# First stage of a two-layer convolution kernel: group statistics one quad later, batch sums between the spectral products, four result places

## The chip, the cores and the metric

The kernel runs on one core of one Trainium2 chip. The metric is the device time of one execution in microseconds (us); smaller is better. Before the change it is 5682.46 us, the median of three runs (5677.47 to 5682.60).

## The reference

`x` is (8, 128, 128, 128) in float32: eight batches of 128 images of 128 by 128. Two layers are computed, each adding to its input a function of the group-normalised input (32 groups of 4 images, so one group is one "quad"):

```python
x = x + filtered_lrelu(gn(x), f)      # layer 0: up by 2 with a 12-tap filter, leaky ReLU, filter and down by 2, in h and w
x = x + spectral(gn(x), a, b, c, d)   # layer 1: rfft2, product of low modes with a tensor-train weight, irfft2
def gn(v):                            # groups of 4 channels
    return (g - mean(g)) / sqrt(var(g) + 1e-5)
```

In layer 1 the kernel takes the mean and the scale of a group from sums over the batch's x1 (the output of layer 0) and puts them into the spectra after the transform.

## The kernel before, in words

There are three phases. The change touches only the first, `phase1`: it computes layer 0 and the forward spectra, and ends at about 3090 us of the span. The second multiplies the modes, the third transforms back and adds.

`phase1` handles one quad per step, 256 steps numbered q, with buffers chosen by k = q mod 8. Each engine has its own instruction list, written out by hand for eight steps (`body`) and looped by `steps`; engines meet only at semaphores, and each works strictly in the order of its list. So whatever one instruction waits for, all behind it on that engine waits too.

In step q TensorE (`step` in the block of `pe`) does, in this order: `up_cols` 0 and 1 of quad q; `down_rows` of quad q-1 (48 matmuls on Y, then six on Yt); `tails` (products with Yb, Yc, At); `up_rows` 0 of quad q+1, which needs g of quad q+1 (`g_ok`); `up_cols` 2 and 3 of q; `up_rows` 1 of q+1; `down_cols` of q-1; and the row transform of x1 of quad q-2 (products with `dfth`). PSUM is a ring of four pairs of banks; `pair_of(k, u)` says which pair the u-th piece uses. I count times of a step from the start of its `down_rows`.

ScalarE (`act`) copies from PSUM: `sloped` (L), `At`, `Yb`, Z high, `high(1)` (Y), Lt, Zt, A high, Yt, `sloped`, `high(3)`, A high, then G. VectorE (`dve`) computes Yf 0 and 1, Yc (`y_tail`), the statistics of x1 (L668), Z low, Zt low, Ytf, A low 0 (L638), Yf 2 and 3, A low 1, x1b (L709). GpSimd (`pool`) does `high(0)`, `low(0)`, `low(1)`, Yt, `high(2)`, `low(2)`, `low(3)`, and then `ground`, which writes g of quad q+2. `low(1)` waits for `high(1)` of ScalarE.

The group statistics of layer 0 are made for four quads at once, a "half" (HALF = 4). In the steps with k mod 4 = 0 and 1, `x_stats` runs bn_stats on x. At the end of k mod 4 = 1, `x_sums` (four small VectorE instructions, L572 to L578) prepares them. In k mod 4 = 2, TensorE sums over partitions (L359, before `tails`), VectorE reads the result (`stats_copy`, L583, before A low 0), forms the variance (`stats_var`, L588 to L592, after Yf 3), ScalarE takes the root (L460), and VectorE writes rstd and nmr (`stats_out`, L598 and L600, after A low 1). `ground` at the end of that step then makes g of the first quad of the next half.

Once per batch (step k = 5 of the last `body` of a batch, s6 given) the statistics of x1 are reduced: `batch_in` (L608 to L615), TensorE's sums L364, `batch_out` (L621 to L632), and after the step `spectra`: 16 units, each of eight matmuls with G (L418, L420), a copy psb by ScalarE (L528), two results by VectorE (L724, L726) into `sp_out`, and two stores of 256 KB by SyncE (L184). `sp_out` has two places; the copy psb waits for `batch_out`.

Of the kernel before, what the change touches and what calls it, by code (L numbers as in the profile page):

```python
# [28 lines left out]
IMGS = 4  # L29
# [11 lines left out]
X_SCALE = 128.0  # L41
# [23 lines left out]
def phase1(nc, x, ut_d, dt_d, dtail_d, mask_d, dfth_d, dftw_d, ones_d, x1, spec):  # L65
    with ExitStack() as ctx:
# [37 lines left out]
        sp_out = sb("sp_out", [128, 2, 2, 4, 128])  # L104
# [19 lines left out]
        sp_st = [sem("sp_st0"), sem("sp_st1")]  # L124
# [43 lines left out]
        def _(sp):  # L168
# [9 lines left out]
            def store_spectra(b):  # L178
                with sp.Fori(0, UNITS6 // 2) as j2:
                    for e in range(2):  # L180
                        j = 2 * j2 + e
# [6 lines left out]
            def first():  # L188
                for e in range(2):
                    sp.sem_inc(sp_st[e], 32)  # L190
# [17 lines left out]
            def drain():  # L208
                store(63, 1)
                store_spectra(B - 1)  # L210
                for e in range(2):
                    sp.wait_ge(x1_st[e], 16 * 33)
                    sp.wait_ge(sp_st[e], 32 + 2 * 16 * B * UNITS6 // 2)
# [4 lines left out]
        def _(pool):  # L218
# [11 lines left out]
            def step(q, k, half=None):  # L230
# [16 lines left out]
                low(1)  # L247
                pool.wait_ge(e_yth, q + 1)
# [4 lines left out]
                if half is not None:  # L253
                    ground(q + 2, k + 2, half)
# [19 lines left out]
        def _(pe):  # L274
# [56 lines left out]
            def step(q, k, up=True, nxt=True, down=True, rows=True, next_half=None, batch=None, after=None):  # L331
                e, o = k % 2, 1 - k % 2
                pr = [pair_of(k, u) for u in range(9)]
                if up:
# [22 lines left out]
                if next_half is not None:  # L357
                    pe.wait_ge(k_mv, next_half + 1)
                    pe.matmul(ring[:, pr[3], 1, 400:400 + 2 * HALF], ones[:], mv[:].rearrange("p q s -> p (q s)"),  # L359
                              start=True, stop=True).then_inc(p_st, 1)  # L360
                if batch is not None:
                    pe.wait_ge(b_x, batch + 1)
                    for s in range(2):
                        mm = pe.matmul(ring[:, pr[3], 1, 500 + s:501 + s], mvx[:, s].rearrange("p q i -> p (q i)"),  # L364
                                       ones[:, 0:1], start=True, stop=True)
                    mm.then_inc(p_st2, 1)
# [16 lines left out]
                if nxt:  # L383
# [15 lines left out]
                if rows:  # L399
                    pe.wait_ge(e_x1, q - 1)  # L400
                    for m in range(IMGS):
                        mm = pe.matmul(ring[:, pr[8], 1, 128 * m:128 * m + 128], x1b[:, (k - 2) % SLOTS, m, :],
                                       dfth[:], start=True, stop=True)
                    mm.then_inc(p_s5, 1)

            def spectra(b, q):
                if q is not None:
                    pe.wait_ge(e_yf, 4 * q + 4)
                    pe.wait_ge(e_al, 2 * q + 4)
                    pe.wait_ge(e_x1, q)  # L410
                pe.wait_ge(e_g, QUADS * (b + 1))
                for j in range(UNITS6):
                    pr = pair_of(5, 9 + j)
                    if j >= 4:
                        pe.wait_ge(e_s6, UNITS6 * b + j - 3)
                    for n in range(4):
# [7 lines left out]
            def first():  # L424
# [8 lines left out]
                for q in range(4):  # L433
                    step(q, q, down=q >= 1, rows=q >= 2, next_half=1 if q == 2 else None)

            def body(t, jq, s6):
                for k in range(8):
                    q = 8 * t + 4 + k
                    step(q, k + 4, next_half=2 * t + 2 + k // HALF if k % HALF == 2 else None,
                         batch=s6 if k == 5 else None, after=s6 if k == 6 else None)  # L440
# [7 lines left out]
            def drain():  # L448
                step(NQ, 0, up=False, nxt=False)
                step(NQ + 1, 1, up=False, nxt=False, down=False, batch=B - 1)  # L450
                pe.wait_ge(b_tot, B)
# [5 lines left out]
        def _(act):  # L457
# [8 lines left out]
            def step(q, k, up=True, nxt=True, down=True, rows=True, j5=None, next_half=None, batch=None):  # L466
# [12 lines left out]
                if up:  # L479
# [3 lines left out]
                    sloped(1, 1)  # L483
                if down:
# [20 lines left out]
                if batch is not None:  # L505
                    act.wait_ge(b_var, batch + 1)
                    act.activation(tt2[:, 4:5], tt2[:, 3:4], ACT.Sqrt, scale=X_SCALE ** 2).then_inc(b_sd, 1)
# [6 lines left out]
                if next_half is not None:  # L514
                    root(next_half)
                if rows:
# [3 lines left out]
                                   ACT.Copy).then_inc(e_g, 1)  # L520

# [9 lines left out]
            def first():  # L531
# [3 lines left out]
                for q in range(4):  # L535
                    step(q, q, down=q >= 1, rows=q >= 2, j5=q - 2, next_half=1 if q == 2 else None)

            def body(t, jq, s6):
                for k in range(8):
                    j5 = jq(k) - 1 if s6 is None else (jq(k) - 1) % QUADS  # L540
                    step(8 * t + 4 + k, k + 4, j5=j5, next_half=2 * t + 2 + k // HALF if k % HALF == 2 else None,
# [16 lines left out]
        def _(dve):  # L558
# [89 lines left out]
            def step(q, k, up=True, nxt=True, down=True, rows=True, j5=None, half=None, loads=1, stored=None,  # L648
# [5 lines left out]

                def yf(m, u):
# [9 lines left out]
                if rows:  # L665
                    dve.wait_ge(e_x1, q - 1)
                    carry(dve, carried[1])
                    dve.bn_stats(st2[:, bass.ds(j5, 1)].rearrange("p o v s -> p (o v s)"),  # L668
                                 x1b[:, (k - 2) % SLOTS].rearrange("p i w -> p (i w)")).then_inc(b_bn, 1)
                if batch is not None:  # L670
                    batch_in(batch)
# [11 lines left out]
                if nxt:  # L683
                    if half is not None and k % HALF == 2:
                        stats_copy(half, pr[3])
                    a_low(q + 1, k + 1, 0, pr[4])
                if batch is not None:
                    batch_out(batch, pr[3])
# [3 lines left out]
                if half is not None:  # L692
                    if k % HALF < 2:
                        x_stats(loads, (k // HALF + 1) % 2, k % HALF)
                    if k % HALF == 2:
                        stats_var(half)
                if nxt:
                    a_low(q + 1, k + 1, 1, pr[7])
                if half is not None:
                    if k % HALF == 1:  # L700
                        x_sums(half)
                    if k % HALF == 2:
                        stats_out(half, (k // HALF + 1) % 2)
                if down:
                    slot = (k - 1) % SLOTS
                    dve.wait_ge(p_s4, q)
                    if stored is not None:
# [3 lines left out]
                                             op0=ALU.mult, op1=ALU.add).then_inc(e_x1, 1)  # L711

            def spectra(b):
                for j in range(UNITS6):
                    dve.wait_ge(sp_st[j % 2], 32 * (8 * b + j // 2 + 1))
# [8 lines left out]
                    dve.scalar_tensor_tensor(out=sp_out[:, j % 2, 0, n0:, :], in0=q_ps[:, n0:, :],  # L724
                                             scalar=rs2[:, 0:1], in1=p_sb[:, n0:, :], op0=ALU.mult, op1=ALU.add)
                    dve.scalar_tensor_tensor(out=sp_out[:, j % 2, 1, n0:, :], in0=q_ps[:, n0:, :],  # L726
# [680 lines left out]
```

## Time and profile before

| | us |
|---|---|
| median of three runs | 5682.46 |
| lowest, highest | 5677.47, 5682.60 |
| profiled execution | 5676.09 |
| its span, first to last instruction | 5673.9 |

| engine | busy us | share of the span |
|---|---|---|
| TensorE matmuls | 4971.0 | 88% |
| TensorE weight loads | 4392.5 | 77% |
| VectorE | 4285.9 | 76% |
| ScalarE | 3400.1 | 60% |
| GpSimd | 2561.0 | 45% |

The busy share is a mean over three different phases. In the first phase what matters is the length of a step and the idle time of TensorE inside it. The mean granted clock of TensorE over the span is 0.955 of full speed, 2.4 GHz; in some stretches it is half of that, 1.2 GHz.

### The profile page before, as it was taken

The numbers are of one execution on the slowest core, as the hardware profiler recorded it, in microseconds if no ns is written. First come the engines' busy times: TensorE is split into PE (matmuls) and PEld (weight loads), VectorE is DVE, ScalarE is ACT, GpSimd is POOL, SyncE is SP. The second block draws the span as 40 slices with busy tenths as digits, with TensorE's granted clock in tenths as the row PEclk, the third lists the DMA queues.
The fourth block names the chain that finished last, engine by engine and source line by source line (L and its number), as shares of the span: only waits on it lengthen the run. The fifth ranks groups of instructions, "written<-read, shape, count | busy, mean of one in ns | idle before, by whom it ended". The sixth has DMA issues, their size and how long they took to land. (4 is left out here: it accounts for less than half of the span.)

```text
span 5673.9 us, 209006 instructions
## 1 busy us (share of the span) xinstructions
PE 4971.0 (88%) x83616; PEld 4392.5 (77%) x83616; DVE 4285.9 (76%) x6708; ACT 3400.1 (60%) x6347; POOL 2561.0 (45%) x2565
## 2 busy tenths in 40 slices
PE   8989989989889899899896499999999999978888
PEld 6877877777777777777786488888888888868888
DVE  7878868878778688788785788888888888862323
ACT  6757757757567577576673266666666666652222
POOL 6747747747567477476572133333333333320000
PEclk9999999999999999999998599999999999988989
DMA  1131131131221311311214022222222222239999
GB/s 53 57 90 51 57 91 50 57 91 50 73 76 50 91 58 50 91 58 55 86 57 138 16 74 74 74 72 70 71 71 71 74 74 74 74 111 347 358 348 321
DMA packets 586295, 553.87 MB, mean 98 GB/s; under 512 B 15028, under 2 KB 540212, under 8 KB 573108
## 3 DMA queue, kind: packets, MB, share of 16 engines
q1 hardware_dynamic: 585780, 546.48, 29.8%
q8 instruction: 387, 6.34, 0.5%
q14 instruction: 128, 1.05, 0.1%
HBM read 277.99 MB, written 268.44 MB: 96 GB/s over the span
## 5 line engine op out<-in xcount | busy, mean ns | idle before, releaser
L1153 DVE TENSOR_TENSOR Ml<-ring,Mh 128x1024 f16<-128x1024 f32 x1024 | 1199.6, 1219 | 200.3 <-ACT Mh L1120 192.7
L243 POOL TENSOR_TENSOR Y<-Yf,Y 128x532 f16<-128x532 f32 x1024 | 1210.3, 1195 | 139.5 <-ACT Y L477 97.3
L1120 ACT ACTIVATE Mh<-ring 128x1024 f16<-128x1024 f32 x1024 | 986.4, 1022 | 320.1 <-PE ring L1054 319.4
L1054 PE MATMUL ring<-wcur,b_hi 64*128 64x128 f16 x16384 | 747.7, 217 | 205.1 <-DVE Ml L1153 138.6
L277 PE MATMUL ring<-uth,A 128*128 128x266 f16 x6144 | 817.0, 283 | 34.0 <-issue 16.9
L1054 PEld LDWEIGHTS ring<-wcur,b_hi 64*128 64x128 f16 x16384 | 609.6, 94 | 275.2 <-DVE Ml L1153 156.3
L658 DVE TENSOR_TENSOR Yf<-ring,L 128x532 f32<-128x532 f32 x1024 | 686.2, 707 | 112.0 <-ACT L L473 99.2
L277 PEld LDWEIGHTS ring<-uth,A 128*128 128x128 f16 x6144 | 612.0, 100 | 191.6 <-issue 29.8
L1054 PE MATMUL ring<-wcur,b_lo 64*128 64x128 f16 x8192 | 715.6, 216 | 0.0
L236 POOL CAST Y<-Yf 128x532 f16<-128x532 f32 x512 | 320.7, 626 | 720.1 <-DVE Yf L658 719.6
L473 ACT ACTIVATE L<-ring 128x532 f32<-128x532 f32 x1024 | 603.4, 606 | 55.5 <-PE ring L277 44.4
L283 PE MATMUL ring<-ut,g 128*128 128x266 f32 x2048 | 598.5, 417 | 3.1 <-POOL g L224 2.9
L638 DVE TENSOR_TENSOR A<-ring,A 128x532 f16<-128x532 f32 x512 | 363.4, 710 | 188.0 <-ACT A L464 177.7
L1079 PE MATMUL ring<-pout,am 128*128 128x256 f32 x2048 | 477.8, 387 | 8.8 <-DVE pout L1161 0.9
L1331 DVE TENSOR_TENSOR xq<-xq,ring 128x512 f32<-128x512 f32 x256 | 172.7, 687 | 413.3 <-DMA xq<-x 212.9
L1067 PE MATMUL ring<-xs,Mh 128*128 128x32 f16 x8192 | 446.1, 177 | 36.7 <-DVE pout L1161 32.9
L1067 PEld LDWEIGHTS ring<-xs,Mh 128*128 128x128 f16 x8192 | 420.4, 96 | 67.7 <-DVE pout L1161 43.9
L477 ACT ACTIVATE Y<-Yf 128x532 f16<-128x532 f32 x512 | 329.5, 643 | 228.2 <-DVE Yf L658 226.2
L277 PE MATMUL ring<-dth,Y 128*128 128x64 f16 (+1 forms) x12288 | 433.2, 196 | 24.2 <-issue 12.5
L277 PEld LDWEIGHTS ring<-dth,Y 128*128 128x128 f16 x12288 | 419.5, 99 | 41.9 <-issue 15.5
L283 PEld LDWEIGHTS ring<-ut,g 128*128 128x128 f32 x2048 | 362.7, 197 | 106.6 <-issue 58.5
L1069 PE MATMUL ring<-xs,Ml 128*128 128x16 f16 x8192 | 440.6, 169 | 0.8 <-issue 0.8
(139 smaller groups left out, 9721.5 us busy)
## 6 DMA issues: line engine op xcount, KB each, us to landing
xb<-in_x SPq DMA_DIRECT2D x128, 512.0 KB, 4.3
x<-x1b SPq DMA_DIRECT2D x64, 1024.0 KB, 6.3
spec<-sp_out SPq DMA_DIRECT2D x256, 256.0 KB, 2.6
xin<-spec SPq DMA_DIRECT2D x128, 512.0 KB, 6.4
fd<-ft SPq DMA_DIRECT2D x128, 512.0 KB, 4.3
F<-fd SPq DMA_DIRECT2D x8, 8192.0 KB, 27.6
xq<-x SPq DMA_DIRECT2D x128, 512.0 KB, 5.3
out<-xq SPq DMA_DIRECT2D x64, 1024.0 KB, 8.4
```

Of the source, the lines that this page charges most:

```text
L243: pool.tensor_tensor(Y[:, e, 1, m], Yf[:, m], Y[:, e, 0, m], ALU.subtract).then_inc(e_yl, 1)
L277: mm = pe.matmul(out, data(v), const(c), start=(start and n == 0), stop=(stop and n == 2), skip_group_check=True)
L283: mm = pe.matmul(ring[:, pr, m, 0:UPS], g[:, k % 2, 2 * n + m, :], ut[:], start=True, stop=True)
L473: act.activation(L[:, m % 2], ring[:, pr[u], :, 0:UPS], ACT.Copy, scale=SLOPE).then_inc(e_l, 1)
L638: dve.tensor_tensor(A[:, k % 2, 1, 2 * n:2 * n + 2, :], ring[:, pr, :, 0:UPS], A[:, k % 2, 0, 2 * n:2 * n + 2, :], ALU.subtract).then_inc( ...
L658: dve.tensor_tensor(Yf[:, m], ring[:, pr[u], :, 0:UPS], L[:, m % 2], ALU.max).then_inc(e_yf, 1)
L1054: mm = pe.matmul(ring[:, UNIT_PAIR[n], t, 128 * k:128 * k + 128], b[r, z, 4 * u + k, :], wcur[r, z, w, :], start=(part == 0), stop=(part = ...
L1067: pe.matmul(o, Mh[:, z, y, :], xs[:, z, y].rearrange("p v r b -> p (v r b)"), start=True, stop=False)
L1069: mm = pe.matmul(o[:, 0:16], Ml[:, z, y, :], xs[:, z, y, 0].rearrange("p r b -> p (r b)"), start=False, stop=True)
L1079: mm = pe.matmul(ring[:, AUX, bank, 256 * z:256 * z + 256], am[:, z, r, C * u:C * u + C], pout[:, z, r, 4 * h:4 * h + 4, :].rearrange("p b ...
L1120: act.activation(hi, ps, ACT.Copy).then_inc(e_hi, 1)
L1153: dve.tensor_tensor(lo, ps, hi, ALU.subtract).then_inc(e_lo, 1)
```

## The change

- Layer 0 statistics. `x_sums` moves from the end of k mod 4 = 1 into k mod 4 = 2, where the statistics of x1 stood (those move behind Yf 3 in that step). TensorE's sums move from before `tails` to before `up_rows` 1, into pair 7. `stats_copy` and `stats_var` move behind A low 1. The root moves to k mod 4 = 3, behind `sloped(1)`, and `stats_out` to k mod 4 = 3, before Z low. `down_rows` of that step waits for `stats_copy`. On GpSimd, `ground` for the first quad of a half moves from the end of step k mod 4 = 2 to the middle of step k mod 4 = 3, behind `low(1)`.
- Batch sums. `batch_in` moves behind Yf 3, `batch_out` to the end of the step; TensorE's sums L364 stand between the first and the second unit of `spectra`; the row transform of that step is put ahead of `down_cols`; the waits at the head of `spectra` are spread over its first units. ScalarE's root goes behind G.
- `sp_out` has four places instead of two, each with its semaphore.

The core of the diff:

```diff
-        sp_out = sb("sp_out", [128, 2, 2, 4, 128])
+        sp_out = sb("sp_out", [128, 4, 2, 4, 128])
@@ pool, step
                 low(1)
+                if half is not None and k % HALF == 3:
+                    ground(q + 1, k + 1, half)
                 pool.wait_ge(e_yth, q + 1)
...
-                if half is not None:
+                if half is not None and k % HALF != 2:
                     ground(q + 2, k + 2, half)
@@ pe, step
+                    if last_half is not None:
+                        pe.wait_ge(k_tot, last_half + 1)
                     down_rows(q, o, pr[2])
...
-                if next_half is not None:
-                    pe.wait_ge(k_mv, next_half + 1)
-                    pe.matmul(ring[:, pr[3], 1, 400:400 + 2 * HALF], ones[:], mv[:].rearrange("p q s -> p (q s)"),
-                              start=True, stop=True).then_inc(p_st, 1)
-                if batch is not None:
-                    pe.wait_ge(b_x, batch + 1)
...
                     if next_half is not None:
-                        pe.wait_ge(k_tot, next_half + 1)
-                    if batch is not None:
-                        pe.wait_ge(b_tot, batch + 1)
+                        pe.wait_ge(k_mv, next_half + 1)
+                        pe.matmul(ring[:, pr[7], 1, 400:400 + 2 * HALF], ones[:],
+                                  mv[:].rearrange("p q s -> p (q s)"), start=True, stop=True).then_inc(p_st, 1)
                     up_rows(q + 1, k + 1, 1, pr[7])
                     pe.wait_ge(e_al, 2 * q + 3)
+                if batch is not None:
+                    row_transform()
                 if down:
...
@@ pe, spectra
-                if q is not None:
-                    pe.wait_ge(e_yf, 4 * q + 4)
-                    pe.wait_ge(e_al, 2 * q + 4)
-                    pe.wait_ge(e_x1, q)
...
+                    elif j == 2:
+                        pe.wait_ge(b_tot, b + 1)
+                    elif j == 1:
+                        if q is not None:
+                            pe.wait_ge(e_al, 2 * q + 4)
+                        pe.wait_ge(b_x, b + 1)
+                        for n in range(2):
+                            mm = pe.matmul(ring[:, pair_of(5, 11), 1, 500 + n:501 + n],
...
+                    if q is not None:
+                        if j < 2:
+                            pe.wait_ge(e_yf, 4 * q + 3 + j)
+                        elif j == 3:
+                            pe.wait_ge(e_x1, q)
@@ act, step
                     sloped(1, 1)
+                if last_half is not None:
+                    root(last_half)
@@ dve, step
-                if batch is not None:
-                    batch_in(batch)
+                sums = half is not None and k % HALF == 2
+                if sums:
+                    x_sums(half)
+                elif rows:
+                    x1_stats()
+                if half is not None and k % HALF == 3:
+                    stats_out(half, (k // HALF + 1) % 2)
                 if down:
...
+                if batch is not None:
+                    batch_in(batch)
+                if half is not None and k % HALF < 2:
+                    x_stats(loads, (k // HALF + 1) % 2, k % HALF)
+                if sums and rows:
+                    x1_stats()
                 if nxt:
                     a_low(q + 1, k + 1, 1, pr[7])
...
+                if sums:
+                    stats_copy(half, pr[7])
+                    stats_var(half)
                 if down:
...
+                if batch is not None:
+                    batch_out(batch, pr[7])
@@ dve, spectra
-                    dve.wait_ge(sp_st[j % 2], 32 * (8 * b + j // 2 + 1))
+                    dve.wait_ge(sp_st[j % 4], 32 * (4 * b + j // 4 + 1))
```

## Rows read from the trace of the kernel before

**Rows 1.** Page, part 1: busy us (share of the span) and instructions of each engine.
```profile
PE 4971.0 (88%) x83616; PEld 4392.5 (77%) x83616; DVE 4285.9 (76%) x6708; ACT 3400.1 (60%) x6347; POOL 2561.0 (45%) x2565
```
**Rows 2.** Timeline, TensorE, one plain step: start, duration, instructions, [idle before <-releaser].
```profile
1117.26 1.63 PE L277 MATMUL ring<-dth,Y 128*128 128x64 f16 x48
...
1119.35 0.35 PE L277 MATMUL ring<-dth,Yb 128*40 128x64 f16 x6 [0.22 <-DVE Yc L645]
...
1120.24 1.16 PE L283 MATMUL ring<-ut,g 128*128 128x266 f32 x4
...
1126.86 1.63 PE L277 MATMUL ring<-dth,Y 128*128 128x64 f16 x48
```
**Rows 3.** Busy time in four steps: stretch, length, engines (x instructions), PEclk, DMA share, GB/s.
```profile
1013.12:1023.88 10.76, 9.70 (x137) 8.29 (x135) 10.03 (x23) 7.64 (x18) 7.37 (x8) 1.00 0.01 2
1023.88:1033.79 9.91, 9.37 (x135) 7.99 (x133) 7.92 (x13) 7.35 (x17) 7.43 (x9) 1.00 0.19 55
162.70:175.40 12.70, 11.56 (x137) 9.04 (x135) 10.48 (x21) 7.31 (x17) 7.41 (x9) 0.87 0.01 1
2931.30:2943.80 12.50, 11.41 (x139) 9.20 (x137) 10.32 (x23) 7.93 (x18) 7.44 (x9) 0.86 0.00 1
```
**Rows 4.** Timeline, TensorE, in the first of those steps.
```profile
1016.38 0.34 PE L277 MATMUL ring<-dth,Yb 128*40 128x64 f16 x6 [1.06 <-issue]
```
**Rows 5.** Busy time in three stretches around a batch's spectra, columns as above.
```profile
1126.86:1187.40 60.54, 45.04 (x395) 41.04 (x393) 34.73 (x63) 19.61 (x38) 8.19 (x10) 0.92 0.50 145
1187.40:1202.06 14.66, 13.88 (x135) 11.00 (x135) 10.28 (x18) 6.09 (x13) 6.67 (x7) 0.65 0.31 85
1202.06:1216.90 14.84, 11.13 (x158) 9.41 (x157) 9.45 (x17) 9.04 (x22) 8.44 (x10) 0.94 0.15 43
```
**Rows 6.** Timeline, TensorE, in those stretches.
```profile
1131.80 0.61 PE L364 MATMUL ring<-ones,mvx 128*128 128x1 f32 x4 [3.07 <-DVE mvx L615]
...
1144.28 0.79 PE L418 MATMUL ring<-dftw,G 128*128 128x128 f32 x2 [3.99 <-DVE x1b L709]
...
1172.23 0.49 PE L418 MATMUL ring<-dftw,G 128*128 128x128 f32 x2 [1.23 <-DVE sp_out L726]
...
1213.96 1.86 PE L277 MATMUL ring<-uth,A 128*128 128x266 f16 x12 [2.64 <-issue]
```
**Rows 7.** Timeline, VectorE: one hole of a plain step, one variance instruction.
```profile
1120.22 1.23 DVE L674 TENSOR_TENSOR Z<-ring,Z 128x1024 f16<-128x1024 f32 x1 [0.52 <-ACT Z L489]
1021.67 1.05 DVE L592 TENSOR_SCALAR var<-var 128x4 f32<-128x4 f32 x1
```
**Rows 8.** Line L592 over the whole run: duration ns min/median/max, first and last start.
```profile
L592 DVE TENSOR_SCALAR var<-var x64: 169/1053/1125, 16.1 to 2981.4; 128x4 f32<-128x4 f32 x64
```
**Rows 9.** Timeline, GpSimd, steps k mod 4 = 2 and 3.
```profile
1021.50 2.35 POOL L243 TENSOR_TENSOR Y<-Yf,Y 128x532 f16<-128x532 f32 x2
1024.16 0.77 POOL L224 TENSOR_SCALAR g<-xb,rstd,nmr 128x512 f32<-128x512 f32 x1 [0.31 <-DVE nmr L600]
...
1027.43 1.20 POOL L243 TENSOR_TENSOR Y<-Yf,Y 128x532 f16<-128x532 f32 x1 [0.21 <-ACT Y L477]
```
**Rows 10.** Timeline, ScalarE: `high(1)` in step k mod 4 = 3, G in a plain step.
```profile
1026.71 0.64 ACT L477 ACTIVATE Y<-Yf 128x532 f16<-128x532 f32 x1
...
1125.69 0.60 ACT L518 ACTIVATE G<-ring 128x512 f32<-128x512 f32 x1 [0.21 <-PE ring L402]
```
**Rows 11.** Who waited for whom, first phase: us in total, times, longest us.
```profile
DVE sp_out L724 <- DMA spec<-sp_out: 136.3, 103, 2.8
```
**Rows 12.** Timeline, VectorE: first and last unit of the last batch's spectra.
```profile
3049.27 0.61 DVE L726 SCALAR_TENSOR_TENSOR sp_out<-ring,rs,psb 128x384 f32<-128x384 f32 x1
...
3086.78 0.74 DVE L726 SCALAR_TENSOR_TENSOR sp_out<-ring,rs,psb 128x512 f32<-128x512 f32 x1
```
**Rows 13.** Busy time in two stretches of spectra, columns as above.
```profile
1150.00:1160.00 10.00, 10.00 (x90) 10.00 (x90) 4.65 (x7) 3.44 (x5) 0.00 (x0) 0.99 0.64 180
...
1170.00:1180.00 10.00, 6.88 (x57) 6.31 (x56) 5.58 (x8) 2.07 (x3) 0.00 (x0) 1.00 0.74 206
```

More of the change, by code:

```diff
@@ L123, in phase1 @@
         x1_st = [sem("x1_st0"), sem("x1_st1")]
-        sp_st = [sem("sp_st0"), sem("sp_st1")]
+        sp_st = [sem(f"sp_st{n}") for n in range(4)]
         g_ok = sem("g_ok")
@@ L178, in store_spectra @@
             def store_spectra(b):
-                with sp.Fori(0, UNITS6 // 2) as j2:
-                    for e in range(2):
-                        j = 2 * j2 + e
+                with sp.Fori(0, UNITS6 // 4) as j4:
+                    for e in range(4):
+                        j = 4 * j4 + e
                         sp.wait_ge(e_s6, UNITS6 * b + j + 1)
@@ L188, in first @@
             def first():
+                for e in range(4):
+                    sp.sem_inc(sp_st[e], 32)
                 for e in range(2):
-                    sp.sem_inc(sp_st[e], 32)
                     sp.sem_inc(x1_st[e], 16)
@@ L212, in drain @@
                     sp.wait_ge(x1_st[e], 16 * 33)
-                    sp.wait_ge(sp_st[e], 32 + 2 * 16 * B * UNITS6 // 2)
+                for e in range(4):
+                    sp.wait_ge(sp_st[e], 32 + 2 * 16 * B * UNITS6 // 4)
             steps(sp, first, body, lambda: store(62, 0), drain)
@@ L329, in down_cols, with step, row_transform @@
                       lambda v: dtailh[:, v, 0:IMGS * TLN], stop=True).then_inc(p_s4, 1)
-            def step(q, k, up=True, nxt=True, down=True, rows=True, next_half=None, batch=None, after=None):
+            def step(q, k, up=True, nxt=True, down=True, rows=True, next_half=None, last_half=None, batch=None,
+                     after=None):
                 e, o = k % 2, 1 - k % 2
                 pr = [pair_of(k, u) for u in range(9)]
+                def row_transform():
+                    pe.wait_ge(e_x1, q - 1)
+                    for m in range(IMGS):
+                        mm = pe.matmul(ring[:, pr[8], 1, 128 * m:128 * m + 128], x1b[:, (k - 2) % SLOTS, m, :],
+                                       dfth[:], start=True, stop=True)
+                    mm.then_inc(p_s5, 1)
                 if up:
@@ L398, in step @@
                     down_cols(o, pr[8])
[L399 to L404, printed above, removed]
+                if rows and batch is None:
+                    row_transform()
             def spectra(b, q):
-                if q is not None:
-                    pe.wait_ge(e_yf, 4 * q + 4)
-                    pe.wait_ge(e_al, 2 * q + 4)
-                    pe.wait_ge(e_x1, q)
                 pe.wait_ge(e_g, QUADS * (b + 1))
@@ L433, in first @@
                 for q in range(4):
-                    step(q, q, down=q >= 1, rows=q >= 2, next_half=1 if q == 2 else None)
+                    step(q, q, down=q >= 1, rows=q >= 2, next_half=1 if q == 2 else None,
+                         last_half=1 if q == 3 else None)
             def body(t, jq, s6):
@@ L464, in a_high, with step @@
                 act.activation(A[:, k % 2, 0, 2 * n:2 * n + 2, :], ring[:, pr, :, 0:UPS], ACT.Copy).then_inc(e_ah, 1)
-            def step(q, k, up=True, nxt=True, down=True, rows=True, j5=None, next_half=None, batch=None):
+            def step(q, k, up=True, nxt=True, down=True, rows=True, j5=None, last_half=None, batch=None):
                 e, o = k % 2, 1 - k % 2
@@ L535, in first @@
                 for q in range(4):
-                    step(q, q, down=q >= 1, rows=q >= 2, j5=q - 2, next_half=1 if q == 2 else None)
+                    step(q, q, down=q >= 1, rows=q >= 2, j5=q - 2, last_half=1 if q == 3 else None)
             def body(t, jq, s6):
@@ L683, in step @@
                 if nxt:
-                    if half is not None and k % HALF == 2:
-                        stats_copy(half, pr[3])
                     a_low(q + 1, k + 1, 0, pr[4])
-                if batch is not None:
-                    batch_out(batch, pr[3])
                 if up:
```

43 lines of the change are left out of this document (15 added, 28 removed).

## The prediction

> **What bounds the kernel now.** I read the page's engine shares first [rows 1]: TensorE leads with 88%, but that is a mean over three phases. So I took TensorE's timeline of single steps of the first phase. A plain step is 9.60 us long, from one `down_rows` (1117.26) to the next (1126.86), and in it TensorE waits once, 0.22 us for Yc [rows 2]. TensorE sets the pace; each idle microsecond that the lists add to it or take from it moves the end by as much.
>
> Then the steps that are longer than that. With k mod 4 = 2 the step took 10.76 us and with 3 it took 9.91 [rows 3]; in the first TensorE idles 1.06 us ahead of `tails` [rows 4], in the second about half as long, because `x_sums` or `stats_var` and `stats_out` have made VectorE late for Yc. In 20 of the 55 such k mod 4 = 2 steps (the two after the start and seven behind spectra left aside) the granted clock also fell to half for a while after this idle time, and the step took 12.5 to 12.7 us; the first and the last of the 20 are shown, with a mean clock of 0.87 and 0.86 [rows 3]. The mean over the 55 is then (35 x 10.8 + 20 x 12.55) / 55 = 11.4 us.
>
> The batch step with its spectra took 60.54 us and the next two 14.66 and 14.84 [rows 5]; by the same reading of all seven the means are 60.1, 13.8 and 13.4 us. In them TensorE waits 3.07 us for `batch_in`, 3.99 us for x1b ahead of the first product, about 1.23 us at every second unit for `sp_out`, and 2.64 us at the loop's end for nothing that the profile shows [rows 6].
>
> **Statistics, step k mod 4 = 2.** `x_sums` leaves the end of the step before, so Yc is on time and the 1.06 us shrink to the plain 0.22. In its new place it meets a hole: VectorE waits 0.52 us there for Z high [rows 7], and x1's statistics have moved away too, together a little over a microsecond. But it is four instructions, and such small ones are stretched: L592 took 169 ns at best and 1053 ns in the median [rows 8], and the one at 1021.67 ended when the first of GpSimd's two `low` instructions (1021.50, 2.35 us for both) was over [rows 7, 9]. The Trainium skill states this in GPSIMD Engine Reference, Specifications: GpSimd's SBUF interfaces are shared with VectorE, with contention for instructions with two SBUF inputs or in a 2-port mode; the trace agrees (169 against 1053 ns). `low(0)` runs from about 1.75 to 2.95 us of the step, so `x_sums`, issued at 1.8, is through at about 3.5 instead of 2.5, and Z low is 0.6 us late; `up_cols` 3 then waits some 0.2 us. TensorE's sums now cost their own time in the stream; the four matmuls of L364 took 0.61 us [rows 6], the two here 0.3. So 9.6 + 0.2 + 0.3 = 10.1 us (bounds 9.8 if nothing is stretched, 10.8 if as now), against 11.4: 1.3 us less, 55 times, 72 us.
>
> `stats_copy` and `stats_var` behind A low 1 push x1b, Yf and Yc back by 1 us, nearly as the old place did; `down_rows` waits for `stats_copy`, which is done half a microsecond before it is wanted. I cost that wait at nothing; if A low 1 were late it would be 0.2 us.
>
> **Statistics, step k mod 4 = 3.** Here is the term that decides. g of the next quad is needed by `up_rows` 0, 2.98 us into the step (1120.24 - 1117.26) [rows 2]. Now it is written at 1024.16, 0.28 us into the step, long before [rows 9]. Afterwards `ground` stands behind `low(1)`. `low(1)` waits for `high(1)` of ScalarE, which stands behind Z high and so behind the end of `down_rows`: in this very step `high(1)` ran 1026.71 to 1027.35 [rows 10] and `low(1)` started at 1027.43, which is 3.55 us into the step, for 1.20 us [rows 9]. With 0.77 us for `ground` g is there at 5.5 us at the earliest, 5.65 with the small lateness of Yf. TensorE waits 5.65 - 2.98, about 2.7 us, in every half, with `up_rows` 0 and all behind it. The Yc wait ahead of it is covered, since g ends later anyway; so are `stats_out` (nmr at about 3.9) and the root. Nothing catches up, for VectorE, ScalarE and GpSimd all wait for TensorE's next results.
>
> Such an idle time also lowers the clock. The waits of 3.07 and 2.64 us were followed by stretches at half of 2.4 GHz in all the cases that I looked at, while 1.06 us did it in 20 of 55. Price: 12.55 - 10.76 = 1.8 us [rows 3], of which a little falls into the idle time itself; I take 1.7. So 9.6 + 2.7 + 1.7 = 14.0 us against 9.9: 4.1 us more, 55 times, 226 us (bounds 2.5 and 5.8 more a step).
>
> **Batch sums.** TensorE no longer waits 3.07 us in the step, nor at half clock behind it. The row transform comes ahead of `down_cols`, so G is no longer behind it: ScalarE's G, 8.4 to 9.0 us into the step [rows 2, 10], releases the first unit at 8.9 us, where it now starts at 17.4 (1144.28 - 1126.86). The second unit waits for `batch_in` and A low 1, which `batch_in` (2.3 us) and the statistics of x push to 11.5, then the sums; it starts at 12.0. `batch_out` is through at about 14, and meanwhile TensorE does units 1 to 3 into free pairs.
>
> **Four result places.** Now VectorE waits for stores 103 times, 136.3 us in all [rows 11], and the last batch took 3086.78 - 3049.27 = 37.5 us from unit 0 to unit 15, 2.50 us a unit [rows 12]. With four places the pace is the slowest of three: TensorE, 90 matmul records in 10 us where nothing holds it and 16 in a unit, 1.79 us [rows 13]; VectorE, two instructions of 0.74 us [rows 12]; and the DMA engines, whose 0.74 busy at 206 GB/s [rows 13] gives 278 GB/s when full, 1.88 us for the 512 KB of a unit, which as they start some units late does not hold TensorE up. Sixteen units thus end at 12.0 + 15 x 1.79 = 38.9, and the next `down_rows` starts at 40.3 instead of 60.1. I add 0.6 for one chance of a half clock: 40.9, 19.2 us less, seven times, 134 us. Bounds: 15 us less (the DMA engines at 2.1 a unit) and 21.
>
> The step behind it loses its half clock (0.65 now [rows 5]) but VectorE comes from unit 15 a microsecond late: 10.7 against 13.8, 7 x 3.1 = 22 us less. The one after gets the wait for g and keeps the 2.64 us: 9.6 + 2.7 + 1.7 + 2.6 = 16.6 against 13.4, 22 us more. The last batch's 37.5 us become 15 x 1.88 = 28.2, and it starts 1.6 earlier: 11 us less. The first half adds 1. Phases two and three are not touched.
>
> **The sum.** -72 + 226 - 134 - 22 + 22 - 11 + 1 = +10 us on the profiled execution's 5676.1 us: 5686. The median of the runs is 6.4 us above that execution, so 5692 us for the median.
>
> **Rivals.**
> 1. The clock stays up. If TensorE, idle 2.7 us, keeps its full speed, 62 x 1.7 = 105 us go away: 5587 us; if it falls in half of the cases, 5640. For it: after 1.06 us it stayed up in 35 of 55 steps. Against it: what followed 2.64 and 3.07. The Trainium skill, TensorE: Matmul & The Clock Gate, Loop structure matters more than you think, gives as the bad pattern a wait for a DMA of 8 us, three times what I expect here; by that alone this rival would hold. The trace speaks against it at 2.64 us.
> 2. The slower side: stores bind. If the DMA engines serve no faster with four places than now (2.5 us a unit, the share of 0.74 being all that such short runs get), the places give nothing: 15 units x 0.72 us x 8 = 86 us come back, 5778 us. It decides from 1.9 us a unit up. For it: the stores of 103 waits [rows 11] all move runs of 512 bytes, and that won't change. Against it: with two places the engines stand idle between stores, which is what the 0.74 shows.
> 3. The half clock lasts twice as long, since idle time is left when it falls: 62 x 1.5 = 93 more, 5785 us. In the trace most falls behind short waits did not.
> 4. The wait for g is not there, because GpSimd gets to `ground` before TensorE needs g. It would take `low(1)` ahead of `high(1)`, which the lists exclude: 5692 - 62 x 4.4 = 5420 us.
>
> **How the numbers follow.** My forecast case 0.58, its own range 5655 to 5730; rival 1 0.18, rival 2 0.12, rival 3 0.10, rival 4 0.02. The range of 8 in 10 leaves out rival 4, the lower half of rival 1 and the far ends of 2 and 3: 5610 to 5770. A measurement of this kernel can tell about 0.2%, 11 us, from no change. The forecast case lies 10 us up and is a difference of two terms of 200 us; of its 0.58 I give 0.15 to faster, 0.17 to no change and 0.26 to slower. With rivals 1 and 4 faster is 0.35, with 2 and 3 slower 0.48; same 0.17.
>
> **What would show it.** In TensorE's timeline, step k mod 4 = 3: a wait of 2.3 to 3 us for POOL g ahead of `up_rows` 0, and a granted clock of 0.5 behind it; step length about 14. Step k mod 4 = 2: no idle time over 0.3 us ahead of `tails`, 10.1 us. VectorE's waits for stores fall to under 30 us, the batch step to 41 us, the DMA share in it towards 0.95. The forecast is wrong if the wait for g is under 1.5 us, if the clock stays up, or if a unit of the spectra takes over 2.1 us.

## The result, and the profile after

| | before, us | after, us |
|---|---|---|
| median of four runs | 5682.53 | 5734.39 |
| lowest, highest | 5677.47, 5693.09 | 5716.86, 5739.02 |
| profiled execution | 5676.1 | 5738.2 |
| its span | 5673.9 | 5736.1 |
| mean granted clock | 0.955 | 0.940 |

The kernel became slower by 0.8%: the ratio after to before is 1.0079 (95% interval 1.0058 to 1.0100), 52 us of the median. Forecast were 5692 us, 10 us more. The difference lies in the first phase: its spectra ended at 3087.5 us of the span before and end at 3146.7 now, 59 of the 62 us by which the spans differ.

The page's first part says little of it. TensorE's share is the same 88%, and it is busy for 54 us more with the same 83616 instructions [rows 1], at a mean granted clock of 0.940 instead of 0.955:
```profile
PE 5025.0 (88%) x83616; PEld 4421.7 (77%) x83616; DVE 4239.8 (74%) x6708; ACT 3396.2 (59%) x6347; POOL 2565.2 (45%) x2565
```
Step by step it becomes plain. Busy time in five stretches of the profile after, each from one `down_rows` to the next, and one stretch in the middle of spectra (columns: stretch, length, busy time and instructions of the engines, granted clock, DMA share, GB/s):
```profile
1045.32:1055.15 9.83, 9.61 (x138) 8.22 (x136) 8.50 (x17) 7.36 (x17) 7.42 (x9) 1.00 0.01 2
1055.15:1070.34 15.19, 12.18 (x136) 9.61 (x133) 8.89 (x18) 7.68 (x18) 8.19 (x10) 0.78 0.12 36
1168.53:1209.51 40.98, 38.86 (x396) 37.05 (x393) 33.30 (x58) 18.64 (x36) 8.27 (x10) 1.00 0.69 201
1209.51:1221.23 11.72, 9.79 (x135) 8.14 (x136) 10.59 (x19) 6.69 (x15) 6.44 (x7) 1.00 0.56 154
1221.23:1239.69 18.46, 12.35 (x135) 9.46 (x133) 9.29 (x19) 8.33 (x19) 8.31 (x10) 0.84 0.13 35
1190.00:1200.00 10.00, 10.00 (x92) 10.00 (x92) 7.43 (x12) 4.04 (x6) 0.00 (x0) 1.00 1.04 288
```
The first is k mod 4 = 2: 9.83 us where it was 10.76 or, at half clock, 12.7 [rows 3]. The second is k mod 4 = 3: 15.19 where it was 9.91, with a mean clock of 0.78. The next three are a batch step and the two behind it, 60.54, 14.66 and 14.84 before [rows 5]. In the last TensorE is busy all the time and the DMA engines move 288 GB/s, against 206 [rows 13].

The long step of k mod 4 = 3, in TensorE's timeline after (start, duration, instructions, idle time before and its releaser):
```profile
1055.15 1.63 PE L281 MATMUL ring<-dth,Y 128*128 128x64 f16 x48
...
1058.03 0.34 PE L281 MATMUL ring<-dth,Yb 128*40 128x64 f16 x6 [1.01 <-DVE Yc L662]
...
1060.98 2.14 PE L287 MATMUL ring<-ut,g 128*128 128x266 f32 x4 [2.00 <-POOL g L226]
1062.91 2.87 PE L281 MATMUL ring<-uth,A 128*128 128x266 f16 x12
1065.57 1.57 PE L287 MATMUL ring<-ut,g 128*128 128x266 f32 x4
...
1070.34 1.63 PE L281 MATMUL ring<-dth,Y 128*128 128x64 f16 x48
```
TensorE waits 1.01 us for Yc, does `tails`, then waits 2.00 us for g, and what follows runs at half clock: `up_rows` 0 takes 2.14 us where a plain step has 1.16 [rows 2]. The granted clock had fallen while TensorE still waited for g (two stretches, columns as above):
```profile
1059.90:1060.90 1.00, 0.00 (x0) 0.00 (x0) 0.74 (x3) 0.00 (x0) 0.95 (x2) 0.50 0.00 0
1060.98:1065.50 4.52, 4.52 (x16) 3.12 (x17) 1.08 (x2) 1.53 (x3) 0.65 (x1) 0.50 0.00 0
```
GpSimd in the same step shows why g is late: it stands behind `low(1)`, as forecast, and comes 5.7 us into the step (1060.09 + 0.76 - 1055.15).
```profile
1057.05 0.63 POOL L238 CAST Y<-Yf 128x532 f16<-128x532 f32 x1 [1.86 <-DVE Yf L681]
1057.76 2.34 POOL L245 TENSOR_TENSOR Y<-Yf,Y 128x532 f16<-128x532 f32 x2
1060.09 0.76 POOL L226 TENSOR_SCALAR g<-xb,rstd,nmr 128x512 f32<-128x512 f32 x1
```
Over the first phase, who waited for whom in the profile after (us in total, times, longest us):
```profile
PE ring L287 <- POOL g L226: 126.2, 63, 2.0
...
PE ring L281 <- DVE Yc L662: 112.2, 229, 1.4
...
DVE sp_out L744 <- DMA spec<-sp_out: 32.9, 37, 2.2
```
The wait for g is there 63 times, 2.0 us each; that for stores fell from 136.3 us to 32.9 [rows 11].

I read the start of every `down_rows` and took mean lengths, in us, by the place of the step. The table has all kernels of this study. "Batch" is the step with the spectra in it, "behind it" and "the next" are the two that follow (they are left out of the first two columns); the last column is where the forward spectra end in the span.

```
kernel            k mod 4=2   k mod 4=3   batch   behind it   the next   end of
                  55 steps    55 steps    7       7           7          spectra
before            11.45        9.96       60.07   13.78       13.44      3087.5
after              9.83       14.98       40.98   11.75       17.98      3146.7
e1_old_stats      11.59        9.96       41.29   10.59       13.57      2928.3
e2_ground_first    9.83       12.38       41.01   11.74       16.35      2992.4
e3_places_only    11.55        9.98       49.42   10.07       13.35      2989.0
e4_early_sums     10.56       10.16       40.95   12.63       13.24      2901.3
e5_fill_both       9.83       12.41       41.12   12.24       14.86      2973.3
e6_fill_tails      9.84       13.27       40.50   12.10       15.88      3046.5
e7_one_less        9.75       10.08       40.90   11.90       14.20      2850.3
```

From before to after that is -1.62 x 55 = -89 us, +5.02 x 55 = +276, -19.1 x 7 = -134, -2.0 x 7 = -14, +4.5 x 7 = +32, the last batch about -11, the other steps of the first phase about -1, and the two later phases +3: 62 us, as the spans differ.

### The profile page after: what moved, and what is told of

Same layout as the page of the kernel before. It is cut to its first block and busy times, and to the rows that moved or that the text cites. A ratio compares the mean times of both kernels' runs of the same rounds, so it can differ in the third digit from the quotient of the medians.

```text
span 5736.1 us, 208861 instructions
## 1 busy us (share of the span) xinstructions
PE 5025.0 (88%) x83616; PEld 4421.7 (77%) x83616; DVE 4239.8 (74%) x6708; ACT 3396.2 (59%) x6347; POOL 2565.2 (45%) x2565
## 5 line engine op out<-in xcount | busy, mean ns | idle before, releaser
L281 PE MATMUL ring<-uth,A 128*128 128x266 f16 x6144 | 866.7, 294 | 23.0 <-issue 17.8
L281 PEld LDWEIGHTS ring<-uth,A 128*128 128x128 f16 x6144 | 635.0, 104 | 204.6 <-issue 36.9
L287 PE MATMUL ring<-ut,g 128*128 128x266 f32 x2048 | 658.6, 450 | 129.2 <-POOL g L226 129.2
L287 PEld LDWEIGHTS ring<-ut,g 128*128 128x128 f32 x2048 | 402.6, 218 | 245.6 <-issue 183.3
L481 ACT ACTIVATE A<-ring 128x532 f16<-128x532 f32 x512 | 309.3, 604 | 276.6 <-PE ring L287 276.2
```

The lines of the kernel that those rows point to most:

```text
L281: mm = pe.matmul(out, data(v), const(c), start=(start and n == 0), stop=(stop and n == 2), skip_group_check=True)
L287: mm = pe.matmul(ring[:, pr, m, 0:UPS], g[:, k % 2, 2 * n + m, :], ut[:], start=True, stop=True)
```

## Experiments

Medians are of four runs of each; the kernel before, run between them on the same chip, had 5685.97 us beside the first four kernels and 5688.41 beside the last three. A ratio is always to the kernel before beside it.

**e1_old_stats.** The kernel after with all statistics of layer 0 at their old places; batch sums and result places stay new.

```diff
@@ pool, step
-                if half is not None and k % HALF == 3:
-                    ground(q + 1, k + 1, half)
...
-                if half is not None and k % HALF != 2:
+                if half is not None:
                     ground(q + 2, k + 2, half)
@@ pe, step, ahead of tails
+                if next_half is not None:
+                    pe.wait_ge(k_mv, next_half + 1)
+                    pe.matmul(ring[:, pr[3], 1, 400:400 + 2 * HALF], ones[:], ...
```

> The changed kernel with the group statistics of layer 0 back in all their old places on all engines; batch sums among the products and four result places stay. My theory (two independent parts, gain in the spectra, loss in the statistics): the step k mod 4 = 3 goes back to about 9.9 us and k mod 4 = 2 to 11.4, the batch step stays at 41, so 5682 - 7 x 19 (batch step) - 7 x 2 (step behind) - 11 (last batch) = about 5525 us, 5505 to 5550. Rival (the short batch step is bought by the new statistics, e.g. because VectorE is less late in the step before): the batch step goes back over 46 us and the time is over 5570.

Measured: 5518.86 us, ratio 0.9713 (0.9695 to 0.9732). The two parts of the change are thus worth 5518.9 - 5686.0 = -167 us (batch sums and places) and 5734.4 - 5518.9 = +215 us (statistics; +219 with each kernel against the one before beside it). By the profiled executions the first part is 157 us; 8 us of what is missing lie in the steps k mod 4 = 2, where with the same statistics the clock fell in 23 of 55 here and in 20 before. Two steps of its profile, k mod 4 = 2 and 3, columns as above, are those of the kernel before again [rows 3]:
```profile
1053.44:1064.20 10.76, 9.70 (x138) 8.29 (x135) 10.03 (x23) 7.62 (x18) 7.39 (x8) 1.00 0.02 4
1064.20:1074.10 9.90, 9.36 (x135) 7.99 (x133) 7.93 (x13) 7.34 (x17) 7.44 (x9) 1.00 0.19 55
```

**e2_ground_first.** The kernel after, with `ground` ahead of `low(1)` instead of behind it.

```diff
@@ pool, step
-                low(1)
                 if half is not None and k % HALF == 3:
                     ground(q + 1, k + 1, half)
+                low(1)
```

> The changed kernel, ground moved one instruction ahead, before low(1), in steps k mod 4 = 3. My theory (TensorE waits for g, and g for low(1)): nmr is done 3.8 us into the step, so g comes at 4.6 instead of 5.8; the wait goes from 2.0 to 0.8 us, 62 x 1.2 = 74 us less, and the half clock after it is shorter or rarer, another 30 to 60: 5620 us, 5595 to 5665. Rival (the order on GpSimd does not matter, the step is long because VectorE is late with x1b, Yf and Yc): no change, over 5715.

Measured: 5579.18 us, ratio 0.9809 (0.9793 to 0.9825), 155 us under the kernel after and 16 us under the range that I had expected; the direction was right, the gain too small. One step k mod 4 = 3 of its profile, TensorE and then the busy times:
```profile
1033.52 0.35 PE L281 MATMUL ring<-dth,Yb 128*40 128x64 f16 x6 [0.96 <-DVE Yc L662]
...
1035.60 1.16 PE L287 MATMUL ring<-ut,g 128*128 128x266 f32 x4 [1.13 <-POOL g L226]
```
```profile
1030.70:1042.22 11.52, 9.44 (x135) 7.99 (x133) 8.75 (x18) 7.51 (x18) 7.41 (x9) 1.00 0.16 47
```
The wait for g is 1.13 instead of 2.00 us. Here `up_rows` 0 takes its 1.16 us, at full clock, and the step 11.5 to 11.6 us. In 22 of the 55 steps the clock fell nevertheless and the step was 1.4 to 3.0 us longer; in the kernel after it fell in all 55. So 0.9 us less of waiting brought 2.6 us a step (14.98 - 12.38), two thirds of it by the clock.

**e3_places_only.** The kernel before with nothing of the change but the four result places.

```diff
-        sp_out = sb("sp_out", [128, 2, 2, 4, 128])
+        sp_out = sb("sp_out", [128, 4, 2, 4, 128])
...
-                    dve.wait_ge(sp_st[j % 2], 32 * (8 * b + j // 2 + 1))
+                    dve.wait_ge(sp_st[j % 4], 32 * (4 * b + j // 4 + 1))
```

> The kernel before with nothing but the four result places. My theory (two places make VectorE wait for the stores, TensorE for VectorE): a unit goes from 2.5 to 1.8-1.9 us, the batch step from 60 to about 50, so 8 x 10 + 7 x 1.5 = 90 us less: 5592 us, 5575 to 5615. Rival 2 of the prediction (the DMA engines serve no faster): 5682 us.

Measured: 5577.56 us, ratio 0.9814 (0.9798 to 0.9831), in the range. The places alone bring 108 us, 10.65 us of a batch step; the new order of the batch sums brings the other 59 (e1). Ten microseconds in the middle of spectra, columns as above:
```profile
1140.00:1150.00 10.00, 10.00 (x92) 10.00 (x91) 8.11 (x12) 3.50 (x6) 0.00 (x0) 1.00 1.03 286
```
TensorE has no idle time and the stores flow at 286 GB/s. Rival 2, that stores of 512-byte runs bind, falls.

**e4_early_sums.** Mends what the first two runs blame: TensorE's sums ahead of `up_cols` 2 into pair 5, `stats_copy` behind Yf 3, variance and `stats_out` around A low 1, root and `ground` at their old places, so that g is early again. The statistics of x1 of that step are put off to the next one (`back=1`).

```diff
@@ pe, step, ahead of up_cols 2
+                    if next_half is not None:
+                        pe.wait_ge(k_mv, next_half + 1)
+                        pe.matmul(ring[:, pr[5], 1, 400:400 + 2 * HALF], ones[:], ...
@@ dve, step, behind Yf 3
+                if sums:
+                    stats_copy(half, pr[5])
...
-                if sums and rows:
-                    x1_stats()
+                if half is not None and k % HALF == 3 and rows:
+                    x1_stats(back=1)
+                if sums:
+                    stats_var(half)
                 if nxt:
                     a_low(q + 1, k + 1, 1, pr[7])
                 if sums:
-                    stats_copy(half, pr[7])
-                    stats_var(half)
+                    stats_out(half, (k // HALF + 1) % 2)
```

> The changed kernel with the statistics in a third arrangement: x_sums where the change has it, TensorE's sums before up_cols 2 (into that piece's bank), stats_copy and stats_var behind Yf 3, the root, stats_out and ground in their old places, and x1's statistics of that step put off to the empty hole before A low 1 of the next step. My theory (only the late g costs): step k mod 4 = 2 stays at 9.8, step 3 goes to 9.9-10.0: 5734 - 62 x 5.0 = 5424 us, 5400 to 5455. Rival (VectorE is too full in k mod 4 = 2, Yc of the next step comes over 1.5 us late and the clock falls again): step 3 stays over 11, time over 5490.

Measured: 5498.98 us, ratio 0.9676 (0.9659 to 0.9692), 75 us above what I expected. Step k mod 4 = 3 became short, 10.16 us; but k mod 4 = 2 took 10.56. TensorE's timeline has an idle time ahead of the next `down_rows`, and VectorE's shows where it comes from:
```profile
1012.67 1.64 PE L279 MATMUL ring<-dth,Y 128*128 128x64 f16 x48 [0.61 <-DVE A L653]
```
```profile
1009.68 1.17 DVE L605 TENSOR_TENSOR var<-tot,sq 128x4 f32<-128x4 f32 x1
1010.88 1.12 DVE L607 TENSOR_SCALAR var<-var 128x4 f32<-128x4 f32 x1
1011.92 0.70 DVE L653 TENSOR_TENSOR A<-ring,A 128x532 f16<-128x532 f32 x1
```
Two instructions on 128x4 take 2.3 us. GpSimd ran, at the same time:
```profile
1009.63 2.35 POOL L245 TENSOR_TENSOR Y<-Yf,Y 128x532 f16<-128x532 f32 x2
```
Each of the two ends with one of GpSimd's two, and so in 63 of 64 steps (medians 1.17 and 1.12 us). A low 1 stands behind them and `down_rows` waits for it. My theory missed this. Its rival named a full VectorE and a time over 5490 us, which came, but in the wrong step: it wanted step k mod 4 = 3 over 11 us.

**e5_fill_both and e6_fill_tails.** These split the price of waiting into its idle time and its clock. Nothing is shortened; TensorE gets needless products in the idle time, which go to a part of PSUM that nobody reads. e5 fills both idle times, e6 only the first, ahead of `tails`.

```diff
+            def filler(pr, n):
+                for _ in range(n):
+                    pe.matmul(ring[:, pr, 1, 300:512], uth[:, 0, 0:128], uth[:, 0, 0:212], start=True, stop=True,
+                              skip_group_check=True)
@@ pe, step, ahead of tails (both)
+                if last_half is not None:
+                    filler(pr[3], 9)
@@ pe, step, ahead of the wait for g (e5 alone)
+                    if last_half is not None:
+                        filler(pr[4], 20)
                     pe.wait_ge(g_ok, q + 2)
```

> The changed kernel with filler matmuls on TensorE in both idle times of step k mod 4 = 3: 9 of 128x212 ahead of tails (into unused columns of that bank) and 20 ahead of the wait for g (into unused columns of the bank of up_rows 0); their results are not used, all waits stay. Theory (of the 5.0 us that step 3 loses, 2.5 are the half clock that the idle time brings, 2.5 the idle time itself): TensorE is as late as now but keeps full speed, step 3 goes from 15.0 to 12.5, 5734 - 62 x 2.5 = 5580 us, 5560 to 5610. Rival (the half clock costs nothing, since TensorE waits for others behind it anyway): 5720 or more.

> As the run with both fillers, but with the 9 filler matmuls ahead of tails alone; the wait of 2.0 us for g stays empty. Theory (the half clock lasts 6.8 us instead of 3.4 in most steps because two idle times follow each other, 1.0 and 2.0 us): it falls still, but mostly for 3.4 us, step 3 goes from 15.0 to about 14.1: 5680 us, 5650 to 5705. Rival (the 2.0 us alone bring the same): over 5715.

Measured for e5: 5571.05 us, ratio 0.9801 (0.9785 to 0.9817), 163 us under the kernel after, with 29 more products in each such step. TensorE, step k mod 4 = 3, and the busy times of that step and of the first phase:
```profile
1038.45 0.99 PE L292 MATMUL ring<-uth 128*128 128x212 f16 x9
...
1040.27 1.99 PE L292 MATMUL ring<-uth 128*128 128x212 f16 x20
1042.41 1.16 PE L287 MATMUL ring<-ut,g 128*128 128x266 f32 x4
1043.41 1.53 PE L281 MATMUL ring<-uth,A 128*128 128x266 f16 x12
```
```profile
1036.65:1049.04 12.39, 12.24 (x165) 10.48 (x163) 8.80 (x18) 7.51 (x18) 7.43 (x10) 1.00 0.15 45
20.00:3000.00 2980.00, 2847.02 (x38079) 2456.77 (x38077) 2418.11 (x4329) 1977.04 (x4295) 1896.50 (x2046) 0.99 0.23 72
```
The same first-phase stretch of the kernel after has a clock of 0.94:
```profile
20.00:3000.00 2980.00, 2698.02 (x34659) 2279.01 (x34658) 2313.35 (x4139) 1905.66 (x4124) 1828.64 (x1972) 0.94 0.21 65
```
The step with g as late as before but the clock up takes 12.41 us on the mean. In none of the 55 did the clock fall; 54 took 12.4 us, and one was 1.2 us longer, with an idle time of 1.05 us for which the profile shows no releaser. The half clock alone cost 14.98 - 12.41 = 2.57 us a step.

Measured for e6: 5639.62 us, ratio 0.9917 (0.9901 to 0.9934), under the range that I had expected. In TensorE's timeline the idle time ahead of `tails` is filled and 2.15 us are left ahead of `up_rows` 0:
```profile
1021.40 0.99 PE L292 MATMUL ring<-uth 128*128 128x212 f16 x9
...
1025.45 1.16 PE L287 MATMUL ring<-ut,g 128*128 128x266 f32 x4 [2.15 <-POOL g L226]
```
```profile
1019.60:1033.74 14.14, 11.99 (x145) 9.71 (x143) 8.90 (x18) 7.69 (x18) 8.21 (x10) 0.88 0.13 38
```
In 27 of the 55 steps the clock fell and the step took about 14.13 us, as this one (mean clock 0.88; here `up_rows` 0 still ran at full speed and what came later did not); in 28 it didn't fall and the step took 12.46 on the mean. One idle time of 2.15 us thus costs 1.67 us in half of the cases.

Two, of 1.01 and 2.00 us with a microsecond of work between them (the kernel after), cost more in every case, and the trace shows how. In 44 of its 55 steps the clock fell while TensorE still waited for g, 0.7 to 1.6 us before the wait was over; there the half clock lasted twice as long as in the other 11, and the step took 15.21 us on the mean, 2.80 over the 12.41 of e5. In the other 11 it fell later, 0.5 us before the end of the wait at the earliest, and the step took 14.06 us, 1.65 over. In e6, with the first idle time filled, it fell behind the wait each time and never lasted twice as long.

**e7_one_less.** e4 with one of the two variance instructions taken out: the 1e-5 is added by the root's bias, and the clamp of the variance at 0 is left out.

```diff
@@ act, root
-                act.activation(std[:], var[:], ACT.Sqrt).then_inc(k_sd, 1)
+                act.activation(std[:], var[:], ACT.Sqrt, bias=epsb[:, 0:1]).then_inc(k_sd, 1)
@@ dve, stats_var
-                dve.tensor_tensor(var[:], tot[:, :, 1], sq[:], ALU.subtract).then_inc(k_m2, 1)
-                dve.wait_ge(k_m2, 2 * h + 2)
-                dve.tensor_scalar(var[:], var[:], 0.0, EPS, ALU.max, ALU.add).then_inc(k_var, 1)
+                dve.tensor_tensor(var[:], tot[:, :, 1], sq[:], ALU.subtract).then_inc(k_var, 1)
```

> The third arrangement (early sums) with one small VectorE instruction less in the variance: the clamp and the added epsilon go, ScalarE's root adds epsilon as its bias. Theory (in that arrangement each of the two last variance instructions waits for one GpSimd instruction of 1.2 us, which makes A low 1 late, and TensorE waits 0.61 us for it ahead of down_rows): one of the two waits goes, step k mod 4 = 2 from 10.56 to 9.85, 5499 - 62 x 0.7 = 5455 us, 5440 to 5475. Rival (the small instructions are slow by themselves, whatever GpSimd does, 0.17 us each): 5490 to 5499.

Measured: 5442.60 us (5436.79 to 5446.43), ratio 0.9574 (0.9558 to 0.9590), in the range and the best of all: 4.3% under the kernel before. VectorE's timeline, and the steps k mod 4 = 2 and 3:
```profile
990.12 0.16 DVE L604 TENSOR_TENSOR sq<-tot 128x4 f32<-128x4 f32 x1
990.32 1.17 DVE L606 TENSOR_TENSOR var<-tot,sq 128x4 f32<-128x4 f32 x1
991.41 0.70 DVE L652 TENSOR_TENSOR A<-ring,A 128x532 f16<-128x532 f32 x1
```
```profile
1025.01:1034.75 9.74, 9.51 (x138) 8.22 (x135) 8.97 (x20) 7.34 (x18) 7.39 (x9) 1.00 0.01 4
1034.75:1044.83 10.08, 9.38 (x136) 7.99 (x133) 8.73 (x15) 7.53 (x17) 7.58 (x10) 1.00 0.18 54
```
One instruction of 1.12 us on four numbers a partition was worth 0.81 us in each step k mod 4 = 2, 45 us in the 55 of the table, and 56 us by the medians of e4 and e7. The rival, that small instructions are slow by themselves, falls: the first of the two still took 1.17 us, the one before it 0.16.

## Why the prediction was right or wrong, point by point

The likeliest case had the mechanism right and its sum 52 us too low by the profiled executions (+10 forecast, +62 measured). By the medians it was 42, since the execution before that was profiled lies 6.4 us under its median and that of after 3.8 above. The measured median lies within the range of 5610 to 5770, which is 160 us wide, but just over the forecast case's own, 5655 to 5730. The sum is a difference of gains and losses of over 200 us each. It left out 50 us of loss in step k mod 4 = 3, 18 in the two steps behind a batch, and 17 of gain in step k mod 4 = 2; with 1 elsewhere that makes the 52. That the kernel came out clearly slower is more than the sum said, which was within the noise of no change; the chances were 0.48 for slower and 0.35 for faster.

- **Step k mod 4 = 3, the term that failed: the price of the half clock.** The prediction had 9.6 + 2.7 + 1.7 = 14.0 us; measured were 14.98. The lateness was right: g came 5.7 us into the step for 5.65 forecast, and the step without the half clock takes 12.41 (e5) for 12.3. The wait for g itself was 2.00 us, under the 2.3 to 3 that I had named as the sign, because 0.8 us of the same lateness was spent in the wait for Yc (1.01 us for the plain 0.22). The price of 1.7 us, taken from one short idle time [rows 3], was 2.6: 0.9 x 55 is the 50 us by which this term (+226 forecast, +276 measured) was too small. "The Yc wait ahead of it is covered" holds for the idle time alone, since the two waits together end with g; for the clock they don't cover each other. Behind both, the half clock lasted twice as long in 44 of 55 steps (price 2.80 us) and once as I had it in 11 (1.65). With the first filled (e6) the price is 1.67 us, my figure, and due only in half of the steps.
- **Step k mod 4 = 2.** Forecast 10.1 us, measured 9.83. `x_sums` is stretched as forecast (its L592, 1.05 us for 128x8, VectorE's timeline after), and ahead of `tails` TensorE waits the plain 0.22 us:
```profile
1047.35 1.05 DVE L592 SCALAR_TENSOR_TENSOR sm<-st,sm 128x8 f32<-128x8 f32 x1
```
```profile
1047.42 0.35 PE L281 MATMUL ring<-dth,Yb 128*40 128x64 f16 x6 [0.22 <-DVE Yc L662]
```
  But the lateness did not reach TensorE with the 0.5 us that I had added for it and for the sums together; the step is only 0.2 us over a plain one. The gain is 89 us for 72.
- **The batch step.** 40.9 us forecast, 40.98 measured, and by the steps that were named: the first unit starts on G 8.8 us into the step (8.9), the sums run at 11.7 (11.5 and a little), in TensorE's timeline after:
```profile
1177.33 0.48 PE L434 MATMUL ring<-dftw,G 128*128 128x128 f32 x2 [0.64 <-ACT G L532]
...
1180.24 0.61 PE L423 MATMUL ring<-ones,mvx 128*128 128x1 f32 x4 [0.86 <-DVE A L655]
```
- **The two steps behind it.** Forecast 10.7 and 16.6 us, measured 11.75 and 17.98. The first of them is itself a step k mod 4 = 2: VectorE comes late from the last unit and finds `x_sums` in its way. TensorE waits 0.39 us for the unit and 1.33 us for Yc, in the profile after:
```profile
1209.51 1.64 PE L281 MATMUL ring<-dth,Y 128*128 128x64 f16 x48 [0.39 <-DVE sp_out L746]
...
1212.71 0.34 PE L281 MATMUL ring<-dth,Yb 128*40 128x64 f16 x6 [1.33 <-DVE Yc L662]
...
1227.24 2.14 PE L287 MATMUL ring<-ut,g 128*128 128x266 f32 x4 [2.00 <-POOL g L226]
...
1237.14 2.75 PE L281 MATMUL ring<-uth,A 128*128 128x266 f16 x12 [2.93 <-issue]
```
  With the old statistics it took 10.59 (e1), as forecast. The second has the wait for g, its half clock (2.14 us again), and 2.93 us at the loop's end, for which I had 2.6. Together 18 us more than forecast. That `x_sums` is what stands in the way is read from the traces; no run moved it alone.
- **The spectra's part as a whole** was right: -134, -22 and -11 make -167 us. By the steps e1 has 7 x (41.29 - 60.07) = -131 and 7 x (10.59 - 13.78) = -22, and the last batch -11; that the medians too differ by 167 is partly luck, since the profiled executions differ by 157. DMA at 288 GB/s when full, forecast 278 from rows 13. Two of the signs named did not come: the waits for stores fell to 32.9 us, not under 30, and the DMA share of the batch step was 0.69, not near 0.95, which it reached only in the middle of the spectra.
- **The rivals.** 1, the clock stays up, was wrong: it fell in 55 of 55. The Trainium skill's example of a bad pattern (TensorE: Matmul & The Clock Gate, Loop structure matters more than you think) is a wait of 8 us. In these traces shorter ones did it too: two of 1.0 and 2.0 us each time, and one of 2.15 us in 27 of 55 steps (e6). 2 fell by e3 and by the 32.9 us of waits for stores. 3, a half clock twice as long because idle time is left when it falls, was true in 44 of the 55 steps, and with its own reason: there the clock fell 0.7 to 1.6 us before the wait for g was over. It had a chance of 0.10 and is most of what the forecast lacked, 0.9 us a step on the mean of the 1.5 it named. "In the trace most falls behind short waits did not" held for single waits. 4 could not be, as its own condition said. Its place, `ground` ahead of `low(1)`, is e2, with 155 us.

Left open: what decides in which of the steps of e2 and e6, alike by their waits, the clock falls, and how early in a wait it falls in the kernel after.

## What to carry to other kernels

Ask of every moved producer when its first reader wants it and what stands ahead of it in its new list: here 0.8 us of work (`ground`) put behind a 1.2 us instruction that itself waits cost 5.0 us in one step, where the rest of the new order had gained 1.6 us in the step before. When you price the clock, look at all idle times of TensorE that lie close together, even where one covers the other on the path: here 1.01 us ahead of 2.00 us raised the price from 1.7 us in half of the steps to 2.6 us in all. Test a change in its parts: its two halves were worth -167 and +215 us, and the statistics at a third place (e4, and e7 with one instruction less) gave a kernel faster than with either the old or the new one.

## What the runs showed of the hardware

- Half clock behind short waits: in none of 55 steps with both idle times filled (e5), in 22 of 55 behind 0.96 and 1.13 us (e2), in 27 of 55 behind 2.15 us alone (e6), in 55 of 55 behind 1.01 and 2.00 us (after). Where it fell well before the second wait was over, it lasted twice as long (44 of 55 in the kernel after, 7 of 55 in e2, none in e6). Products that nobody reads, 3.0 us of them a step, made the kernel 163 us faster than the same kernel without them.
- Some small VectorE instructions lasted until GpSimd's running one was over, and the next one until the next: 1.17 and 1.12 us for 128x4 (e4), while one issued before GpSimd's two TENSOR_TENSOR began took 0.16 (e7, L604). Not all do: L615 on 128x4, with one SBUF input, took 0.15 us beside a running TENSOR_TENSOR (at 1058.30 in the kernel after; 0.15 to 0.18 in all of its 64 executions).
- The Trainium skill, GPSIMD Engine Reference, Specifications, says that GpSimd's SBUF interfaces are shared with VectorE, and names as contending the VectorE instructions with two SBUF inputs or in a 2-port mode. The trace agrees for L605 of e4, the subtraction of two SBUF tiles. L607, which has one SBUF input, took 1.12 us, and no run shows in which mode it ran.
- Stores in runs of 512 bytes reached 286 to 288 GB/s at a DMA share of 1.03 to 1.04 (e3, after).
